# The first body in another order: three low parts, two masked key tiles and one query sum change place

## The reference

```
x = x + L0_xattn(layernorm(x), ctx)   # 16 heads of 16, softmax over 64 keys, then relu(out @ W1 + b1) @ W2 + b2
x = x + L0_ffn(layernorm(x))          # top 2 of 8 experts: sum_e gate_e * (relu(h @ wi.T + bi + lora_e) @ wo.T + bo)
x = x + L1_xattn(layernorm(x), ctx)   # one head: softmax(q @ k.T) @ v
x = x + L1_ffn(layernorm(x))          # h @ weight.T + (sum of groups of 64 columns) @ disha
```

## Time and profile before

| | us |
|---|---|
| median of three runs | 320.92 |
| the profiled execution's own time | 320.74 |
| its span in the trace | 318.7 |
| TensorE busy | 307.6 |
| VectorE busy | 237.8 |
| ScalarE busy | 169.1 |
| GpSimd busy | 161.3 |

### The profile page before, as it was taken

The page is one execution under the profiler, slowest core; times in us unless marked ns, Lnnn a source line. Parts: engine busy times, 40 slices in busy tenths (PEclk is TensorE's granted clock), DMA queues, the critical chain, the costliest instruction groups (busy, mean ns, idle before and its releaser), DMA issues.

```text
span 318.7 us, 6483 instructions
## 1 busy us (share of the span) xinstructions
PE 307.6 (97%) x2485; PEld 282.8 (89%) x2485; DVE 237.8 (75%) x650; ACT 169.1 (53%) x345; POOL 161.3 (51%) x155
## 2 busy tenths in 40 slices
PE   8999999999999999999999999999999999999972
PEld 6778897999989998999999998999899989999961
DVE  4898775967896878877795789678868679455765
ACT  4347656673475357545746456635753574434520
POOL 1674773794065705572386308560557053803551
PEclk9999999999999999999999999999999999999996
DMA  8693430013010330215021400042012200000001
GB/s 246 189 408 123 135 100 2 0 43 106 19 11 10 81 118 2 16 44 140 20 16 26 140 35 17 2 99 101 3 15 51 82 4 0 2 33 2 0 33 34
DMA packets 15902, 20.02 MB, mean 63 GB/s; under 512 B 2912, under 2 KB 11872, under 8 KB 15616
## 3 DMA queue, kind: packets, MB, share of 16 engines
q1 hardware_dynamic: 14320, 16.57, 19.1%
q10 hardware_dynamic: 1552, 3.05, 2.7%
HBM read 11.48 MB, written 2.63 MB: 44 GB/s over the span
## 4 chain that ended last, share of the span: by engine, by line
PE 82%; DVE 6%; ACT 5%; DMA 3%; POOL 1%; issue 1%; ACTq 0%; POOLq 0%
PE psI L326 14%; PE psI L504 14%; PE psP L335 11%; PE psI L335 10%; PE psS L335 6%; PE psT L326 4%; DMA raw_w<-in_w 3%; PE psP L439 2%; PE psS L412 2%; PE psT L571 2%; PE psS L382 2%; PE psP L440 2%; PE psT L350 2%; PE psP L669 1%; PE psS L326 1%
## 5 line engine op out<-in xcount | busy, mean ns | idle before, releaser
L1570 POOL TENSOR_TENSOR rs<-ve,mhalf 128x2 f32<-128x2 f32 x30 | 21.9, 729 | 97.0 <-DVE ve L1166 97.0
L1589 POOL TENSOR_TENSOR hid_l<-r,hid_h 128x512 fp32r<-128x512 f32 x32 | 42.2, 1330 | 16.7 <-ACT hid_h L950 16.6
L945 ACT ACTIVATE r<-psI,first 128x256 f32<-128x256 f32 x60 | 25.1, 475 | 20.0 <-PE psI L504 20.0
L504 PE MATMUL psI<-at_h,lb_h 128*128 128x256 f32 x120 | 35.1, 292 | 0.0
L1259 DVE SCALAR_TENSOR_TENSOR r<-psI,nbi,r 128x256 f32<-128x256 f32 x60 | 26.1, 477 | 11.4 <-PE psI L504 11.4
L504 PE MATMUL psI<-at_l,lb_h 128*128 128x256 f32 x120 | 33.8, 282 | 0.0
L504 PE MATMUL psI<-at_h,lb_l 128*128 128x256 f32 x120 | 33.7, 281 | 0.0
L1583 POOL TENSOR_TENSOR hs_l<-hs,hs_h 128x512 fp32r<-128x512 f32 x16 | 21.0, 1312 | 21.7 <-ACT hs_h L930 20.9
L1200 DVE RECIPROCAL rec<-psP 128x256 f32<-128x256 f32 x16 | 28.0, 1752 | 1.2 <-PE psP L440 1.2
L876 ACT ACTIVATE xn<-xmid,nmr,rs 128x256 f32<-128x256 f32 x16 | 8.8, 594 | 38.0 <-POOL nmr L1574 38.0
L914 ACT ACTIVATE ex<-psS 128x512 f32<-128x512 f32 x30 | 17.1, 599 | 17.5 <-PE psS L412 15.8
(11 more groups left out here) (293 smaller groups left out, 877.2 us busy)
## 6 DMA issues: line engine op xcount, KB each, us to landing
stack<-qu_h SPq DMA_DIRECT2D x56, 64.0 KB, 2.0
xin<-in_x SPq DMA_DIRECT2D x8, 256.0 KB, 2.8
stack<-qu_l SPq DMA_DIRECT2D x28, 64.0 KB, 2.0
out<-x ACTq DMA_DIRECT2D x7, 256.0 KB, 2.0
xn<-in_xt SPq DMA_DIRECT2D x5, 256.0 KB, 2.9
raw_wi<-in_wi SPq DMA_DIRECT2D x1, 1024.0 KB, 7.4
raw_wo<-in_wo SPq DMA_DIRECT2D x1, 1024.0 KB, 11.0
kv<-in_kv SPq DMA_DIRECT2D x2, 384.0 KB, 6.3
```

The source lines that it names most:

```text
L504: last = mm(bank[:, k * T:(k + 1) * T], (WH, WL)[x]["lb"][:, 0, f * P:(f + 1) * P], AT[y][:, which, :], start=False, stop=q == 2, skip_gro ...
L945: last = A(R1[:, f, :], bank[:, k * T:(k + 1) * T], ACT.Relu, bias=cols[:, BI + f:BI + f + 1])
L1570: G_.tensor_tensor(rs[:, :], ve[:, :], mhalf[:, :], ALU.pow).then_inc(S(f"ln{j}_rs"), 1)
L1589: G_.tensor_tensor(HL[:, two, :], R1[:, two, :], as32(HH[:, two, :]), ALU.subtract).then_inc(S("hidl"), 1)
```

## The change

- VectorE no longer makes the low part of W1 in the opening. GpSimd makes it, between its two writes of head indicators.
- GpSimd's two `kb` tiles of the second batch, made in the opening before, are made at the end of the first body (`second_masked`), after `xr` and ahead of the low parts of `lb` and `wo`.
- The values of batch 1 are made later: on TensorE after the maxima are taken off, on VectorE after the heads' output. TensorE's transposes of block 1 wait for VectorE's first step on them.
- `query_means` (L608) moves from before the values' products to after them. On VectorE the copy of its result and the four `kd` tiles move behind the low part of the transposed block 1.
- The first half of `a_hidden` runs ahead of block 1's transposes, and three filler matmuls go.
- The turn of the maxima (L391) runs after the first piece of the scores instead of after the second.
- The high part of W2 moves on ScalarE to right behind the exponentials, its low part on GpSimd ahead of the heads' low parts.
- Semaphore counts are renumbered to fit.

```diff
             def a_hidden(b, u):
                 if u == 0:
                     if b == 0:
-                        pe.wait_ge(S("lo_w"), 2)
+                        pe.wait_ge(S("lo_wp"), 1)
...
                     if a == 0:
                         a_scores(a, 3)
-                        query_means()
+                        values(T_(1)[:, 0:D], kv0, 1).then_inc(S("v0_ps"), 1)
                     a_attend(a, 0)
...
                 if a == 0:
                     values1()
+                    query_means()
+                if A_:
+                    a_hidden(a, 0)
+                if a == 0:
                     pe.wait_ge(S("v0"), BATCH)
                     transposes(1, h, T_(1))
-                    filler(I_(0), 3)
-                if A_:
-                    a_hidden(a, 0)
...
             opening_scores(0)
+            a_max_transposes(0)
             opening_scores(1)
-            a_max_transposes(0)
             opening_scores(2)
             opening_scores(3)
-            values(T_(1)[:, 0:D], kv0, 1).then_inc(S("v0_ps"), 1)
...
                     exps(a, 3)
+                    if a == 0:
+                        high_weights("w2")
                     normalise(1, h, XIN)
...
                     high(1, h, XTA, T_(1))
-                    high_weights("w2")
                     high_weights("wi")
...
                 if a == 0:
-                    dve.wait_ge(S("centred"), 1)
-                    V.tensor_copy(wqm[:, :], T_(0)[:, D:2 * D]).then_inc(S("centred"), 1)
-                    diagonal(kd_h, kt0_h, "kd_h")
-                    diagonal(kd_l, kt0_l, "kd_l")
+                    first_values(1, T_(1)[:, 0:D])
...
                     low(1, h, XTA, T_(1))
+                if a == 0:
+                    dve.wait_ge(S("centred"), 1)
+                    V.tensor_copy(wqm[:, :], T_(0)[:, D:2 * D]).then_inc(S("centred"), 1)
+                    diagonal(kd_h, kt0_h, "kd_h")
+                    diagonal(kd_l, kt0_l, "kd_l")
...
             first_values(0, T_(0)[:, 0:D])
-            low_weights("w1")
-            first_values(1, T_(1)[:, 0:D])
             dve.wait_ge(S("nbi"), 1)
...
+                if a == 0:
+                    low_weights("w2", 0, 1)
                 if A_:
                     attended_low(a, 0)
                     attended_low(a, 1)
...
-                if a == 0:
-                    low_weights("w2", 0, 1)
...
                 if a == 0:
+                    second_masked()
                     pool.wait_ge(S("crow_ps"), 1)
                     low_weights("lb", 0, 1)
                     low_weights("wo", 0, 2)
...
+            def second_masked():
+                pool.wait_ge(S("kt0_h"), KC)
+                for m in range(KC):
+                    last = G_.tensor_tensor(
+                        KB[:, KC + m, :].rearrange("p (h k) -> p h k", h=8),
+                        as32(kt0_h[:, m * P + KEYS:(m + 1) * P]).unsqueeze(1).broadcast_to([P, 8, KEYS]),
+                        kmask.unsqueeze(2).broadcast_to([P, 8, KEYS]), ALU.mult)
+                last.then_inc(S("kb1"), 1)
...
             indicators(0)
             pool.wait_ge(S("ks_ind"), 1)
+            low_weights("w1", 0, 1)
+            pool.wait_ge(S("lo_wp"), 1)
             indicators(1)
             pool.wait_ge(S("ks_ind"), 2)
```

More of the change, by code:

```diff
@@ L455, in a_out @@
                 if b == 0 and half == 0:
-                    pe.wait_ge(S("lo_wp"), 1)
+                    pe.wait_ge(S("lo_wp"), 2)
                 parts = [(P_(1)[:, t * D:(t + 1) * D], x_of(HS, t * P, P), w("w2", 0, D)) for t in range(NT)]
@@ L467, in f_gate @@
                 if b == 0:
-                    pe.wait_ge(S("lo_w"), 4)
+                    pe.wait_ge(S("lo_w"), 3)
                 if h is not None:
@@ L486, in f_base @@
                     if b == 0:
-                        pe.wait_ge(S("lo_wp"), 2)
-                        pe.wait_ge(S("lo_w"), 3)
+                        pe.wait_ge(S("lo_wp"), 3)
+                        pe.wait_ge(S("lo_w"), 2)
                     else:
@@ L510, in f_first @@
                     if b == 0:
-                        pe.wait_ge(S("lo_wp"), 3)
+                        pe.wait_ge(S("lo_wp"), 4)
                     pe.wait_ge(S("atl"), b + 1)
@@ L523, in f_out @@
                     if b == 0:
-                        pe.wait_ge(S("lo_wp"), 5)
+                        pe.wait_ge(S("lo_wp"), 6)
                     pe.wait_ge(S("hidh"), (b + 1) * NDF)
```

## The result

| | before | changed |
|---|---|---|
| median, us | 320.81 (6 runs, 320.5 to 321.3) | 322.42 (6 runs, 322.05 to 322.53) |
| profiled execution's span, us | 318.7 | 320.4 |

The ratio is 1.0036, with a 95% interval of 1.0019 to 1.0054: slower by 1.6 us, where 322.7 us and +1.8 were forecast.

What follows compares the result with a forecast made beforehand. TensorE, 97% busy, was taken as the bound, with VectorE and ScalarE also in the chain up to 56 us. 320.74 + 0.2 + 0 + 1.6 = 322.54, and 0.18 for the median: 322.7 us, range 320.9 to 323.7.

Steps and rivals of the forecast that it cites:

- Part 1: Opening of the first body: products with the exponentials begin at 20.1 instead of 21.33, heads' output 1.2 us earlier.
- Part 2: Front up to the relu: later transposes, then wi's high part, use up the gain; relu 30.75 against 30.55, +0.2 us.
- Part 3: Key copies and stacked queries' DMAs: 2.1 us later, with 0.6 us slack before the scores' load; cost nothing.
- Part 4: End of first body: GpSimd's two moved tiles get VectorE's srtd held, so TensorE waits for am; +1.6 us.
- rival A: At srtd: the top-2 choice's small operations slip past GpSimd, so not slower, 320.8 us; chance 0.13.
- Rival B: At the relu: the front's 1.2 us survive, the relu not waiting for wi's copy; 321.3 us; chance 0.06.
- rival C: On TensorE: its 1.6 us stand and one before 32 us bring its clock down; 324.7 us; chance 0.04.
- rival D: At the scores: stacked queries land after 49.6, over 2 us later than counted; +0.5 to +1.5, 323.7 us; chance 0.03.

Runs made afterwards that it cites:

- e4: e1 with ScalarE's high part of wi ahead of its copy of transposed block 1, and VectorE's key copies ahead of block 1's low part: 319.66 us, ratio 0.9967.
- e3: The changed kernel with GpSimd's two masked key tiles behind the low parts of lb and wo: 321.87 us, ratio 1.0035.
- e5: The changed kernel run again without an edit, for its spread: 322.66 us, ratio 1.0036.
- e1: The changed kernel with GpSimd's two masked key tiles moved behind the heads' low parts of block 0, into idle time: 321.85 us, ratio 1.0026.

## Why the prediction was right, and where it was off

**Part 1, the heads' output.** Right in kind, short in size: 1.48 us were gained, not 1.2. The term that differs is the gap at the change of tile shape. Loads of the timeline that answers to the earlier trace rows:

```profile
15.86 0.11 PEld L391 LDWEIGHTS psP<-first,mx 128*64 128x64 f32 x1 [0.30 <-DVE mx L1197]
...
18.21 0.53 PEld L405 LDWEIGHTS psS<-stack,ks 16*128 16x128 f32 x4
...
19.34 0.73 PEld L623 LDWEIGHTS psT<-kv 96*128 96x128 f32 x4
...
20.40 0.18 PEld L439 LDWEIGHTS psP<-ex,v 128*32 128x32 f32 x8 [0.33 <-issue]
```

The stall ahead of the turn was 0.30 us, 0.35 said, and the scores end at 18.08 - 0.54 = 17.54, 17.55 said. Between the score products' last load (17.89 + 0.19) and L405 there were 0.13 us, where I took the 0.33 from another pair of shapes. With the offset the products with the exponentials begin at 19.86, not 20.1.

**Part 2, the gain used up.** The mechanism held: ScalarE idles 2.29 us until the transposes arrive, and then wi's high part stands in front of the relu. The relu came at 30.42 against 30.75 said: 0.26 us of that is part 1's, the rest is spread over part 2. The balance was -0.03 us against the recorded start 30.45; the +0.2 was taken against the chain's 30.55, which is clipped, and against 30.45 it would have read +0.3. e4 shows the mechanism from the other side.

**Part 3, the key copies.** 2.1 us later were said and 31.66 - 0.54 - 29.08 = 2.04 measured. The stack's last DMAs slipped a little more, from 43.83 to 46.67 - 0.54, 2.3 us. I counted 0.6 us of slack. By the 1.56 to 1.58 us that e3, e4 and e5 need from the end of the last issue to the load, the changed kernel with its 48.35 - 46.67 = 1.68 us had about 0.1 (an estimate from these traces). In the changed kernel it cost nothing, because the wait of part 4 lies behind it, as the prediction had it.

**Part 4, the hold.** Right by mechanism, place and size. The tiles took 2.24 us beside `ga_l`'s remainder; `am` ends 1.65 us later with the offset taken off (50.43 - 0.54 - 48.24), 1.66 said (49.9 - 48.24), and the lora's first product stands 1.56 us later, 1.6 said. Its parts were the ones named: `srtd` +2.02 us, less 0.33 of the copy's own wait. The general sentence behind it, that VectorE's operations on SBUF alone are held whatever their size, is too wide: see the last section. The rule of the Trainium skill cited there (SBUF — State Buffer, Terms), under which the loser is blocked for the whole instruction, now has its row: 16 columns held 2.02 us. e3's conversion and e1's short `srtd` put rival A to rest.

**The sum.** -0.03 + 0 + 1.6 from the traces, against +0.2 + 0 + 1.6; the median moved by 1.61. The forecast of 322.7 was 0.3 us high: 0.2 are part 2's balance, 0.1 the median before, 320.92 over three runs and 320.81 over six. Rival B fell with the relu's start, rival C with the clock line of the changed kernel's page, which reads 9 in all slices but the last, through a TensorE wait of 1.6 us. Of rival D's lateness, over 2 us, no run showed more than a 0.30 us wait (e5), under cover.

## What to carry to other kernels

Before an operation is moved into a stretch where GpSimd "has time", look at what VectorE has on the critical path there, not only at GpSimd's queue. A chain of tiny copies, subtractions and conversions on SBUF is a bad neighbour of long GpSimd operations, since each can be held for the rest of one; put long GpSimd work where VectorE waits or reads PSUM. In the changed kernel four operations with one operand from PSUM (`crow`, `kt`, `v`, `xtf_l`) ran beside the masked tiles and the start of `lb_l`, from 41.63 to 43.78, in 0.41, 0.41, 0.68 and 0.69 us, and in 0.41, 0.41, 0.67 and 0.69 before. And a gain ahead of an in-order queue is worth only what the next item of that queue lets through: find the item, and move it into the idleness that the gain has made.

## What the runs showed of the hardware

Not every VectorE operation on SBUF is held. In e3 the two `MAX8` ran beside the first tile (0.23 us for both; none of the run's sixteen took over 0.17) and the two `FIND_INDEX8` beside the second (0.15 us each, where the median of the sixteen is 0.16), while the subtraction between them and the conversion behind them were held by the same tiles. A type conversion of 16 columns was held as well (e3, 0.68 us against 0.17). So was a multiplication of two columns by a constant, with GpSimd in a one-input operation on 16 partitions that ends at 20.34; but the product of two SBUF tensors at 17.91, which ran beside the same operation, took 0.98 us against 0.43, and was through long before it ended. In the changed kernel:

```profile
17.58 2.76 POOL L1706 TENSOR_SCALAR ks<-first 16x1024 fp32r<-16x1024 f32 x1
...
17.91 0.98 DVE L1506 TENSOR_TENSOR v<-v,vrows 128x256 f32<-128x256 f32 x1
...
19.87 0.50 DVE L1166 TENSOR_SCALAR nm<-mv 128x2 f32<-128x2 f32 x1
```

and in e1:

```profile
16.61 2.76 POOL L1707 TENSOR_SCALAR ks<-first 16x1024 fp32r<-16x1024 f32 x1
...
17.24 0.68 DVE L1506 TENSOR_TENSOR v<-v,vrows 128x256 f32<-128x256 f32 x1
```

By the hold seen elsewhere, and by the rule of the Trainium skill cited in part 4 (SBUF — State Buffer, Terms), the product should have lasted until 20.34. The measurement decides otherwise, and in a regular way: in all eight traces with this pair the product ends 1.31 or 1.32 us after the GpSimd operation's start (17.91 + 0.98 - 17.58, and 17.24 + 0.68 - 16.61), whether it began 0.33 us behind it or 0.63. So its end goes by the start of that operation and not by its own. Why is open; no run was made for it.
